# First layer of a two-layer graph network: adjacency blocks turned by a transposing DMA in place of TensorE transposes

## The reference, cut to what matters

```
x, adj = 3327 x 256 f32, 3327 x 3327 of 0.0 and 1.0 (diagonal 1)
h = relu(layernorm(x))
A = (adj != 0);  hidden = h @ W0 + b0;  deg = sum(A, axis=0)
x = x + (A @ hidden) / deg[:, None]                       # first layer
h = relu(layernorm(x))
# second layer: S = adj + I, row- and column-normalised; two steps of
#   Xf = Rf @ Xf;  Xb = Rb @ Xb;  Xa = nucleus_softmax(Q W2 K^T) @ Xa
#   Z += Xf @ U1 + Xb @ U2 + Xa @ U3
x = x + layernorm(h + Z) * gamma + beta
```

## Time and profile before

| | before |
|---|---|
| runs | 2170.18, 2171.49 us (median 2170.84) |
| profiled execution, first to last instruction | 2168.8 us |
| around the span, against the two runs | 1.4 and 2.7 us |
| PE busy | 1888.8 us (87%) |
| DVE busy | 1654.5 us (76%) |
| ACT busy | 1252.7 us (58%) |
| DMA engines in the first layer (100 to 200 us) | 81.6% (60.8% loads, 20.8% stores) |
| first convolution starts | 37.16 us |
| store of strip 24 issued, after its diagonal was added | 281.60 us |

### The profile page before, as it was taken

One profiled execution on the slowest core, in us unless ns is written; L12 is line 12 of the kernel. 1 busy time (PEld: TensorE's weight loads), 2 busy tenths in 40 slices (PEclk: granted clock), 3 DMA queues, 4 the chain that ended last, 5 costly groups with the idle time before them and its releaser, 6 DMA issues.

```text
span 2168.8 us, 38810 instructions
## 1 busy us (share of the span) xinstructions
PE 1888.8 (87%) x12312; PEld 1413.3 (65%) x12312; DVE 1654.5 (76%) x4204; ACT 1252.7 (58%) x2027; POOL 331.3 (15%) x764
## 2 busy tenths in 40 slices
PE   3999964599999999999568359999999999999997
PEld 3999942477777777777447136666666666666665
DVE  5222262888888888888885189999999999999997
ACT  4222244566666666666342376767768677776852
POOL 3000121000000000000000003222231322313130
PEclk9999987799999999999788779999999999999999
DMA  6787712101111111111010301011010100101022
GB/s 152 175 175 176 178 52 99 35 30 42 45 45 45 45 45 44 42 30 41 22 42 10 105 20 39 19 39 36 22 39 19 39 24 34 38 20 39 19 100 66
DMA packets 59758, 123.92 MB, mean 57 GB/s; under 512 B 13635, under 2 KB 45761, under 8 KB 59456
## 3 DMA queue, kind: packets, MB, share of 16 engines
q1 hardware_dynamic: 50144, 96.99, 13.2%
q0 software_dynamic: 3744, 22.14, 6.7%
q10 hardware_dynamic: 5824, 4.26, 0.6%
HBM read 107.99 MB, written 37.49 MB: 67 GB/s over the span
## 4 chain that ended last, share of the span: by engine, by line
DVE 35%; PE 28%; DVEq 13%; ACT 13%; issue 10%; DMA 1%; ACTq 1%; POOL 0%; POOLq 0%; SPq 0%
DVE scraps L1236 8%; DVE stats L1350 6%; DVE window L1236 5%; PE lg L965 4%; PE bank L910 4%; PE lg L910 3%; ACT turned L765 3%; ACT turned L767 3%; ACT expo L748 3%; DVEq L1531 3%; PE bank L1031 3%; PE bank L1010 3%; PE bank L985 2%; DVE window L1393 2%; DVEq L1397 2%
## 5 line engine op out<-in xcount | busy, mean ns | idle before, releaser
L1010 PE MATMUL bank<-xcur,probs_t 128*128 128x256 f32 x2704 | 592.2, 379 | 0.0
L1010 PEld LDWEIGHTS bank<-xcur,probs_t 128*128 128x128 f32 x2704 | 509.8, 190 | 67.2
L801 ACT ACTIVATE probs_t<-bank 128x512 f32<-128x512 f32 (+1 forms) x364 | 190.1, 564 | 247.7 <-PE bank L999 246.5
L999 PE MATMUL bank<-ident,window 128*128 128x128 f32 x1352 | 200.8, 290 | 131.1 <-DVE kept_inv L1533 117.3
L999 PEld LDWEIGHTS bank<-ident,window 128*128 128x128 f32 x1352 | 150.4, 145 | 230.7 <-DVE kept_inv L1533 141.1
L985 PE MATMUL bank<-both,s_tile 128*128 128x512 f16 x1352 | 300.1, 379 | 0.0
L1221 DVE TENSOR_SCALAR_CACHE_REDUCE expo<-lg 128x1024 f32 (+1 forms) x208 | 205.0, 1022 | 62.4 <-PE lg L965 51.9
L965 PE MATMUL lg<-k_t,q_tile 64*128 64x512 f32 (+1 forms) x832 | 197.2, 574 | 53.6 <-DVE expo L1221 25.2
L767 ACT ACTIVATE turned<-expo,found 128x3327 uint8<-128x3327 f32 x78 | 239.6, 3071 | 5.3
L765 ACT ACTIVATE turned<-expo,found 128x3327 uint8<-128x3327 f32 x78 | 239.3, 3068 | 3.7
L1350 DVE MAX8 stats<-window 128x8 f32<-128x208 f32 (+1 forms) x780 | 238.9, 384 | 0.0
(11 more groups left out here) (266 smaller groups left out, 2485.6 us busy)
## 6 DMA issues: line engine op xcount, KB each, us to landing
s_tile<-s_scratch SPq DMA_DIRECT2D x52, 832.0 KB, 4.5
expo<-in_adj POOLq DMA_DIRECT2D x25, 831.8 KB, 9.0
s_scratch<-s_tile SPq DMA_DIRECT2D x14, 832.0 KB, 8.8
s_scratch<-probs_t SPq DMA_DIRECT2D x6, 832.0 KB, 8.9
s_scratch<-window SPq DMA_DIRECT2D x6, 832.0 KB, 9.2
x_scratch<-both SPq DMA_DIRECT2D x1, 3328.0 KB, 9.5
q_tile<-q_scratch SPq DMA_DIRECT2D x104, 32.0 KB, 2.1
xa_scratch<-ht ACTq DMA_DIRECT2D x26, 128.0 KB, 1.7
```

The costliest lines, as they stand in the source:

```text
L801: A.activation(probs_t[:, k0 * P:(k0 + n) * P], flip_ps[g % 2][:, 0:n * P], ACT.Copy).then_inc(p_moved[s], 1)
L999: last = T.transpose(flip_ps[g % 2][:, k * P:(k + 1) * P], window[:, (k0 + k) * P:(k0 + k + 1) * P], ident[:, :])
L1010: last = T.matmul(pv_ps[:, 0:D], probs_t[:, k * P:(k + 1) * P], xcur[:, k, :], start=(k == 0), stop=(k == NT - 1))
```

## The change

SP's queue issues one transposing DMA for each strip, which reads `natural[b]` and writes the 26 turned blocks to `s_buf[q]`, and counts `s_turned[b]` up when it has landed. The flips on PE, the two PSUM banks' part in them and the copies by DVE and ACT are gone, with their semaphores. The count stays on PE, at k = 14 in place of k = 12. The load of strip t now waits until strip t - 2 has been counted and turned. SP's loop is written out strip by strip.

```diff
-FLIP_AT = (12, 14, 18, 21)
+COUNT_AT = 14
...
-            def store_s(tile):
-                t, _, _, _, q = tile
+            def turn_s(t):
+                b, m, q = t % 2, t // 2, t % 4
+                sp.wait_ge(nat_in[b], DMA * (m + 1))
+                sp.wait_ge(s_stored[q], DMA * (t // 4 + 1))
+                sp.dma_start_transpose(s_buf[q][:, :, :], natural[b][:, :]).then_inc(s_turned[b], DMA)
+
+            def store_s(t):
                 sp.wait_ge(s_made, t + 1)
-                sp.dma_start(dram_tile(s_dram, t), flat(s_buf[q][:, :, :])).then_inc(s_stored[q], DMA)
-            with sp.Fori(0, NT // 4) as i:
-                for j in range(4):
-                    store_s(at(i, j))
-            for j in range(NT % 4):
-                store_s(at(NT // 4, j))
+                sp.dma_start(dram_tile(s_dram, t), flat(s_buf[t % 4][:, :, :])).then_inc(s_stored[t % 4], DMA)
+            turn_s(0)
+            turn_s(1)
+            for t in range(NT):
+                if t + 2 < NT:
+                    turn_s(t + 2)
+                store_s(t)
...
             def load_adj(t, m, b):
-                pool.wait_ge(adj_flipped, (t - 1) * NA + 8)
+                if not isinstance(t, int) or t >= 2:
+                    pool.wait_ge(counted, t - 1)
+                    pool.wait_ge(s_turned[b], m * DMA)
...
-            def move_flipped(tile, g):     # ACT, and the same on DVE with tensor_copy for even g
-                t, _, _, c, q = tile
-                k0, n = ADJ_GROUPS[g]
-                if g == 1:
-                    act.wait_ge(s_stored[q], DMA * (c + 1))
-                act.wait_ge(adj_flipped, t * NA + g + 9)
-                A.activation(flat(s_buf[q][:, k0:k0 + n, :]), flip_ps[1][:, :].bitcast(BF16)[:, 0:n * P], ACT.Copy).then_inc(adj_moved_s, 1)
...
-            def flip(tile, g):
-                t, _, b, _, _ = tile
-                k0, n = ADJ_GROUPS[g]
-                pe.wait_ge(adj_moved_s if g % 2 else adj_moved_v, t * (NA // 2) + g // 2 + 1)
-                view = flip_ps[g % 2][:, :].bitcast(BF16)
-                for k in range(n):
-                    last = T.transpose(view[:, k * P:(k + 1) * P], natural[b][:, (k0 + k) * P:(k0 + k + 1) * P], ident_bf[:, :])
-                last.then_inc(adj_flipped, 1)
 
             def convolve(tile, after, first=False):
-                t, _, b, _, q = tile
-                pe.wait_ge(adj_moved_v, (t + 1) * (NA // 2) + 1)
-                pe.wait_ge(adj_moved_s, (t + 1) * (NA // 2) + 1)
+                t, m, b, _, q = tile
+                pe.wait_ge(s_turned[b], DMA * (m + 1))
```

More of the change, by code:

```diff
@@ L64 @@
 LOGITS_LATE = list(range(min(2, NL), NL))
-FLIP_ADJ = 8
-ADJ_GROUPS = [(k, min(FLIP_ADJ, NT - k)) for k in range(0, NT, FLIP_ADJ)]
-NA = len(ADJ_GROUPS)
 TEAM = 4
@@ L290, in graph_layers @@
         s_stored = [sem(f"s_stored_{n}") for n in range(4)]
-        adj_flipped = sem("adj_flipped")
-        adj_moved_v = sem("adj_moved_v")
-        adj_moved_s = sem("adj_moved_s")
+        s_turned = [sem(f"s_turned_{n}") for n in range(2)]
+        counted = sem("counted")
         conv_out = sem("conv_out")
@@ L326, in graph_layers @@
             *[(s_stored[n], DMA) for n in range(4)],
-            (adj_flipped, 8),
-            (adj_moved_v, 1),
-            (adj_moved_s, 1),
             (conv_out, 1),
@@ L681, in convolve @@
                     turned_out(t - 1)
-                if after is not None:
-                    for g in range(1, NA, 2):
-                        move_flipped(after, g)
                 act.wait_ge(conv_done, t + 1)
@@ L689, in convolve @@
                     multiplied_weights()
-            for g in range(1, NA, 2):
-                move_flipped(at(0, 0), g)
             convolve_all(act, convolve)
@@ L881, in count_columns @@
                 for k in range(NT):
-                    T.matmul(lg[0][:, k:k + 1], natural[b][:, k * P:(k + 1) * P], ones_bf[:, :], start=False, stop=True,
-                             skip_group_check=True)
-            def flip(tile, g):
-                t, _, b, _, _ = tile
-                k0, n = ADJ_GROUPS[g]
-                pe.wait_ge(adj_moved_s if g % 2 else adj_moved_v, t * (NA // 2) + g // 2 + 1)
-                view = flip_ps[g % 2][:, :].bitcast(BF16)
-                for k in range(n):
-                    last = T.transpose(view[:, k * P:(k + 1) * P], natural[b][:, (k0 + k) * P:(k0 + k + 1) * P], ident_bf[:, :])
-                last.then_inc(adj_flipped, 1)
+                    last = T.matmul(lg[0][:, k:k + 1], natural[b][:, k * P:(k + 1) * P], ones_bf[:, :], start=False, stop=True,
+                                    skip_group_check=True)
+                last.then_inc(counted, 1)
             def convolve(tile, after, first=False):
-                t, _, b, _, q = tile
-                pe.wait_ge(adj_moved_v, (t + 1) * (NA // 2) + 1)
-                pe.wait_ge(adj_moved_s, (t + 1) * (NA // 2) + 1)
+                t, m, b, _, q = tile
+                pe.wait_ge(s_turned[b], DMA * (m + 1))
                 for k in range(NT):
@@ L904, in convolve @@
                         project(t - 1)
-                    if after is not None and k == FLIP_AT[0]:
+                    if after is not None and k == COUNT_AT:
                         count_columns(after)
-                    if after is not None and k in FLIP_AT:
-                        flip(after, FLIP_AT.index(k))
                     for part in range(2):
@@ L918, in _ @@
             count_columns(at(0, 0))
-            for g in range(NA):
-                flip(at(0, 0), g)
             convolve_all(pe, convolve)
@@ L1092, in _ @@
             dve.wait_ge(weights_in, DMA * 5)
[L1095 to L1101, removed]
             def projected_out(t):
@@ L1115, in convolve @@
                     projected_out(tile[0] - 1)
-                for g in range(0, NA, 2):
-                    move_flipped(after, g)
                 with_loops(tile)
-            for g in range(0, NA, 2):
-                move_flipped(at(0, 0), g)
             convolve_all(dve, convolve)
```

## The result

The changed kernel took 2243.89 us (2243.11 and 2244.67) against 2170.84: ratio **1.033 [1.031, 1.035]**, slower. All of it happens in the first layer. Its end is where DVE copies the column counts out of PSUM.

What follows compares the result with a forecast made beforehand. PE bounds the first layer before, the DMA engines after: 26 loads (152.4 us), 25 turns of 7 us, some 22 stores (44 us) and a convolution (8.2 us) give a span of 2282 us; forecast 2284 us, range 2160 to 2800.

Steps and rivals of the forecast that it cites:

- PE bounds the layer, 1.46 us of flips per strip: First layer before: PE sets 9.64 us a strip; without flips PE alone could go at 8.18 us.
- DVE's and ACT's copies are worth nothing: First layer: their PSUM copies stand nowhere in the chain of waits, so removing them gains nothing.
- DMA engines become the bound: First layer after: a strip asks 14.9 us of the DMA engines, 5.2 us over today's pitch; DMA share above 90%.
- T = 7 us: Time one strip's turn takes of the 16 DMA engines: geometric mean of 3.75 and 13.3 us.
- Span = 2107 + 25 T: Whole kernel's span, T being one turn's time on the DMA engines: 2282 us with T = 7.
- 1.78 us free per strip: First layer before: DMA engine time left for something new, loads and stores taking 7.86 us of 9.64.
- The loop of load and turn is hidden by the DMA sum at 9.2 us a strip: POOL's order, load and turn of one buffer in succession: 9.2 us a strip, below the DMA engines' 14.9.
- PE's clock: PE waits about 6.7 us per strip; if its clock fell, a strip takes up to 14 us, beside DMA's 14.9.
- Rival A: First layer's turn costs like a copy, T below about 4 us; 2125 to 2190 us, about 2160; chance 24%.
- Rival C: First layer's 26 blocks go one after another at a fixed price, DMA engines idle; 2296 to 3284 us; chance 27%.

Runs made afterwards that it cites:

- plain_four_buffers: Changed kernel with four buffers for loaded strips and a plain DMA of the same bytes in place of the transposing one; first layer ends at 251.67 us.
- no_load: Changed kernel without the loads of strips 2 to 25, two buffers turned again and again; first layer ends at 243.3 us.
- twelve_by_dma: Kernel before, with the last 12 of a strip's 26 blocks turned by DMA and 14 flipped on PE; 2157.6 us, ratio 0.994.

## Why the prediction was right, and where it was off

- **PE bounds the layer, 1.46 us of flips per strip:** right. Where the third transfer is harmless (`plain_four_buffers`) a strip takes 8.2 us, the 8.18 of the prediction, and the layer ends 33 us earlier. Forecast were up to 45 with the start; 36.5 without. In `no_load`, where the turns fit beside PE, it ends 41.5 us earlier, 5.4 of them at the start (first convolution at 31.81 us).
- **DVE's and ACT's copies are worth nothing:** right as far as is seen: the chain before, from 37 to 285 us, holds no such copy. No run removes them alone.
- **DMA engines become the bound:** right. DMA share over 90% was asked for, and it is 111%. The share alone doesn't prove it, since `plain_four_buffers` has 103% at PE's pace; the sum of 11.4 us against strips of 11.7 does.
- **T = 7 us:** 6.4 us over the kernel by the records, but 4.5 us where nothing waits and 4.8 in the last six ordinary strips. I had 3.75 us from rows of 256 bytes and 13.3 from pieces of 32 bytes and took the middle between them. The pieces are the rows of 256 bytes, 3328 of them, and alone they cost 4.5 us, 21 ns each in place of 18. The lower of the two sums was the right one. What lifts the mean to 6.4 lies beside the turn, which the prediction did not have: it priced T as a property of the transfer.
- **Span = 2107 + 25 T:** the form held, two of its terms were mis-sized. A load stands in it at 5.86 us, a share read as a price; it is 4.8. The turn stands at 7, and is 4.5. With both put right the sum gives a span of 2194 us, 49 less than the 2243.0 measured. The two long strips are 31 of these 49, and no term of the prediction stands for them; the other 18 are not split up. So it is partly luck that 2284 came within 40 us: terms that were too large covered slow strips that were not foreseen. The 1.78 us free per strip was too little for the same reason, as `twelve_by_dma` shows.
- **The loop of load and turn is hidden by the DMA sum at 9.2 us a strip:** half right. The chain shows this loop, and its pieces of 11.7 and 10 to 13 us give 11 to 12 us a strip, the 11.7 of the 18 ordinary strips. But its pieces are long because the transfers share the engines, whose own sum is 11.4; loosening it made things worse. What it gave with T = 7, 9.2 us, came from loads of 9.4 us where they take 11.7.
- **PE's clock:** the granted clock from 100 to 200 us is 0.83 in the changed kernel, 1.00 before. The strip that starts at 162.14, after 3.2 us of waiting, begins at the lower of the two levels (1.2 and 2.4 GHz), 0.61 us a pair, with 0.39 again at 164.93. As forecast it hides in the wait. The forecast's "up to 14 us" for a whole strip at the lower level does not follow from its 0.59 us a pair, which is a pair's duration and gives 15.3 us for 26; successive pairs start about 0.46 us apart there, 12 us for 26, which with the strip's other pieces comes near 14. The first convolution started at 32.33 us in place of 37.16, as was allowed for.
- **Rival A (cost of a copy), and the Trainium skill's "Advanced Engine Details and Errata", section X-Bar Transpose (TRN2), by which transposing DMAs are about as fast as regular ones:** fails. Its T had to be below about 4 us and is 4.5. Alone a turn lands in 5.8 us against 3.8 for a store of the same bytes, and moves some 217 GB/s where a store moves 406; beside the kernel's loads single ones take 26 to 32 us.
- **Rival C (block after block):** fails as priced. 26 blocks alone land in 5.8 us, 0.22 us each, not 0.58 or more. The Trainium skill's "VectorE: DVE Perf Modes", section The three transpose paths, gives 1309 ns for one block by DMA; for blocks in a row the trace does not agree. The same page's advice to use TensorE where PSUM will do (section Rules for kernel authors) was right here against turning all blocks by DMA, and not against turning 8 or 12 of the 26.

## What to carry to other kernels

A transposing DMA is priced with its neighbours, not by itself: 4.5 us of the engines for 852 KB alone or beside a plain store, by the records 5 to 14 beside converting loads from GpSimd's queue. Before work is moved to the DMA engines, read how much of their time is free per step, but don't take a queue's share for its price: the load read 5.8 us before and took 4.2 to 4.8 elsewhere. Then move a part and keep the bigger part where it was; a third to a half of the blocks gained 0.6% where all of them lost 3.3%. When a chain alternates between two transfers on one buffer, a further buffer helps only if the engines that carry them have time left: try it before believing the chain.

## What the runs showed that I had not expected

- Four buffers moved less than two: from 60 to 260 us 138 GB/s, against 181 and 189 in the two profiles of the changed kernel. With load and turn kept apart it is 185, no more than with them side by side.
- Single turns of 16 to 32 us in the middle of others of 10 to 14, the slowest at strips 8 and 16 in both profiles of one kernel. What makes them is open.
- SP's queue is held by a turn for 3.9 us (alone) to 14.6 us (beside loads; 17.1 in the second profile, 26.1 with four buffers), where a store of the same bytes holds it for 0.33 us (`plain_four_buffers`) to 0.8 us (the changed kernel).
